# Eight small layers on one core: group routing in pieces inside the feed-forward, a norm's root on another engine, constants made in an earlier phase

## The reference

```python
# layer 1 feed-forward: 16 experts in 4 groups of 4, best 2 groups, best 4 experts
logits = xf @ router_w.T
scores = sigmoid(logits)
sb = scores + correction_bias
group_scores = top_k(sb.reshape(S, 4, 4), 2)[0].sum(-1)
group_idx = top_k(group_scores, 2)[1]
masked = where(score_mask > 0, sb, -inf)
topk_idx = top_k(masked, 4)[1]
w = take_along_axis(scores, topk_idx); w = w / (w.sum(-1) + 1e-20)
combine = zeros((S, 16)).at[arange(S)[:, None], topk_idx].add(w)
h = silu(xf @ gate_w) * (xf @ up_w)          # every expert, 32 columns each
out = shared + einsum('esh,ehc->sc', h * combine.T[:, :, None], down_w)

# layer 3 feed-forward: 8 experts, best 2, softmax of their probabilities
probs = softmax(x @ router); weights, indices = top_k(probs, 2); norm = softmax(weights)
```

## Time and profile before

| | us |
|---|---|
| median of 3 runs (lowest, highest) | 2025.56 (2020.61, 2027.13) |
| the profiled execution | 2014.69 |
| its span, first to last instruction | 2012.9 |
| TensorE busy, of the span | 1589.8 (79%) |
| VectorE busy | 1136.1 (56%) |
| ScalarE busy | 843.5 (42%) |
| GpSimd busy | 564.3 (28%) |

### The profile page before, as it was taken

The page is one execution under the profiler, slowest core; times in us unless marked ns, Lnnn a source line. Parts: engine busy times, 40 slices in busy tenths (PEclk is TensorE's granted clock), DMA queues, the critical chain, the costliest instruction groups (busy, mean ns, idle before and its releaser), DMA issues. The chain is left out here.

```text
span 2012.9 us, 46758 instructions
## 1 busy us (share of the span) xinstructions
PE 1589.8 (79%) x16783; PEld 1167.5 (58%) x16783; DVE 1136.1 (56%) x3048; ACT 843.5 (42%) x1634; POOL 564.3 (28%) x782
## 2 busy tenths in 40 slices
PE   4788999999488879699987776888887588353992
PEld 3655666666256647478875554555554488242882
DVE  5745677777445448356644576876674343552434
ACT  2422455555211115334432344655554476001763
POOL 4111011111101103422212211133233355374554
PEclk9989899999699989799997987998897799555996
DMA  4000222221099200000001002222220242221224
GB/s 173 1 2 10 65 57 61 55 55 44 8 286 328 91 0 1 1 3 3 3 3 64 1 1 58 66 68 66 64 71 21 64 113 86 71 74 45 78 78 144
DMA packets 84684, 124.99 MB, mean 62 GB/s; under 512 B 17329, under 2 KB 70577, under 8 KB 82929
## 3 DMA queue, kind: packets, MB, share of 16 engines
q1 hardware_dynamic: 75824, 104.30, 17.8%
q0 software_dynamic: 8640, 17.78, 2.5%
HBM read 67.47 MB, written 55.59 MB: 61 GB/s over the span
## 5 line engine op out<-in xcount | busy, mean ns | idle before, releaser
L1527 DVE TENSOR_REDUCE small<-ps 128x8 f32<-128x1024 f32 (+1 forms) x256 | 312.5, 1223 | 120.8 <-PE ps L1313 70.4
L1454 ACT ACTIVATE scr<-ps 128x1024 f32<-128x1024 f32 x256 | 262.0, 1023 | 239.7 <-PE ps L1288 121.2
L244 POOL TENSOR_TENSOR rstd<-vare,neghalf 128x4 f32<-128x4 f32 (+1 forms) x72 | 63.2, 878 | 543.6 <-DVE vare L223 542.2
L2826 POOL DMA_INDIRECT results<-scr x142 | 135.9, 957 | 143.8 <-DVE scr L2815 59.3
L1326 PE MATMUL ps<-scr 128*32 128x256 f32 x2048 | 174.0, 414 | 0.2 <-ACT scr L1454 0.2
L1275 PEld LDWEIGHTS ps<-scr_r 32*128 32x128 f32 x1024 | 82.3, 195 | 156.0 <-ACT scr L1454 88.8
L1275 PE MATMUL ps<-scr_r 32*128 32x256 f32 x1024 | 136.3, 344 | 35.8 <-ACT scr L1454 21.8
L2746 PE MATMUL ps<-scr 128*128 128x128 f32 x1136 | 153.4, 279 | 1.3 <-ACT scr L2773 1.3
L1306 PE MATMUL ps<-scr_r 32*128 32x256 f32 x1024 | 137.8, 351 | 10.0 <-DMA scr_r<-scr_r 5.5
L2746 PEld LDWEIGHTS ps<-scr 128*128 128x128 f32 x1136 | 141.9, 196 | 1.6 <-issue 1.6
L1911 PE MATMUL ps<-scr 64*64 64x64 f32 x4480 | 120.0, 223 | 13.3 <-DVE scr L2201 7.1
(11 more groups left out here) (410 smaller groups left out, 3547.7 us busy)
## 6 DMA issues: line engine op xcount, KB each, us to landing
scr_r<-scr_r SPq DMA_DIRECT2D x512, 64.0 KB
rows_m<-kinds SPq DMA_DIRECT2D x8, 2064.0 KB, 30.2
rows_f<-kinds SPq DMA_DIRECT2D x8, 2064.0 KB, 74.7
scr<-results SPq DMA_DIRECT2D x32, 256.0 KB
scr<-rows_m SPq DMA_DIRECT2D x71, 64.5 KB
scr<-rows_f SPq DMA_DIRECT2D x71, 64.5 KB
scr<-in_l3m SPq DMA_DIRECT2D x1, 3072.0 KB, 11.1
results<-scr POOLq DMA_INDIRECT x142
```

The costliest lines, as they stand in the source:

```text
L244: pool.tensor_tensor(k.rstd[:, 0:self.J], k.vare[:, 0:self.J], k.neghalf[:, 0:self.J], ALU.pow).then_inc(self.e["rstd_ready"].sem, 1)
L1454: act.activation(PT[:, g % 2, 2 * x:2 * x + 2, :], ps[:, 4:6, :], ACT.Exp).then_inc(e["prob_ready"].sem, 1)
L1527: dve.tensor_reduce(nf[:, half, 0:blocks, at:at + 2].rearrange("p q a -> p a q"), ps[:, 2 * (p % 2):2 * (p % 2) + 2, :].rearrange("p a (q ...
L2826: pool.indirect_dma_start(results, bass.IndirectOffsetOnAxis(ap=names[:, j % IN, P:P + 1], axis=0), y[:, j % OUT, :], None).then_inc(store ...
```

## The change

1. `phase_route_groups` and its phase are gone. A class `GroupRoute` does the same steps for one block of four tiles, in six pieces c=0 to 5. Block 0 is routed at the start of VectorE's part of the feed-forward, ahead of `make_spare`; block it+1 piece by piece behind the chunks of block it. The one sigmoid over all logits stays, and is now the first thing of ScalarE's part; it writes into `k.combine`, and the routing overwrites the scores there with the weights. GpSimd's `widen` waits for `routed` of its block.
2. Between the experts, `RootNorm` takes the place of `Norm`: ScalarE makes the square root, VectorE its reciprocal, in place of GpSimd's `pow`. On VectorE, normalise of block b moves from behind the names to right behind `choose` of block b-1.
3. The constants of the second `Dispatch` are made by VectorE inside the first expert phase, at tile 32, in place of the start of the stage between.

```diff
+class RootNorm(Norm):
+    def act_root(self, act, it):
+        k = self.k
+        act.wait_ge(self.e["var_ready"].sem, self.e["var_ready"].at(it))
+        act.activation(k.rstd[:, 0:self.J], k.vare[:, 0:self.J], ACT.Sqrt).then_inc(self.e["rstd_ready"].sem, 1)
+    def normalise(self, dve, it):
+        k = self.k
+        dve.wait_ge(self.e["rstd_ready"].sem, self.e["rstd_ready"].at(it))
+        dve.reciprocal(k.vare[:, 0:self.J], k.rstd[:, 0:self.J])
+        dve.drain()
+        if begun(it):
+            dve.wait_ge(self.e["turned"].sem, self.e["turned"].at(it - 1))
+        for j in range(self.J):
+            ins = dve.tensor_scalar(self.out(it, j), self.rows(it, j), k.mv[:, j, 0:1], k.vare[:, j:j + 1],
+                                    ALU.subtract, ALU.mult)
+        ins.then_inc(self.e["xn_ready"].sem, 1)
 # phase_ffn
     def act(act):
+        if route:
+            route.act(act)
     def dve(dve):
         def body(it, late):
                 if beside:
                     beside.dve(dve, it, c)
+                if route and it + 1 < NBLK:
+                    route.dve(dve, it + 1, c)
+        if route:
+            dve.wait_ge(k.arrive["l1f"], 16)
+            dve.wait_ge(route.scores_ready, 1)
+            for c in range(chunks):
+                route.dve(dve, 0, c)
         if begin:
             begin(dve)
     def widen(pool, it):
+        pool.wait_ge(route.e["routed"].sem, route.e["routed"].at(it))
         for c in range(routed):
-def phase_route_groups(k):
+class GroupRoute:
+    def act(self, act):
+        act.activation(self.k.combine[:, :, :], self.k.logits[:, :, :], ACT.Sigmoid).then_inc(self.scores_ready, 1)
+    def dve(self, dve, b, c):
+        k, sb, marked, won, top8, total, gs = self.k, self.sb, self.marked, self.won, self.top8, self.total, self.gs
+        score = k.combine[:, 4 * b:4 * b + 4, :]
+        if c == 0:
+            dve.tensor_tensor(sb, score, row4(k.w["l1f"]["bias"]), ALU.add)
+            dve.drain()
+            dve.tensor_tensor(self.hi, four[:, :, 0:2], four[:, :, 2:4], ALU.max)
+            dve.tensor_tensor(self.lo, four[:, :, 0:2], four[:, :, 2:4], ALU.min)
+            dve.drain()
+            dve.tensor_tensor(self.best, self.hi[:, :, 0:1], self.hi[:, :, 1:2], ALU.max)
+            dve.tensor_tensor(self.least, self.hi[:, :, 0:1], self.hi[:, :, 1:2], ALU.min)
+            dve.tensor_tensor(self.second, self.lo[:, :, 0:1], self.lo[:, :, 1:2], ALU.max)
+            dve.drain()
+        if c == 1:
+            dve.tensor_tensor(self.least, self.least, self.second, ALU.max)
+            dve.drain()
+            dve.tensor_tensor(gs.rearrange("p n g -> p (n g)"), self.best.rearrange("p n a -> p (n a)"),
+                              self.least.rearrange("p n a -> p (n a)"), ALU.add)
+            dve.drain()
+            dve.tensor_tensor(self.d1, gs[:, :, 0:3], gs[:, :, 1:4], ALU.is_ge)
+            dve.tensor_tensor(self.d2, gs[:, :, 0:2], gs[:, :, 2:4], ALU.is_ge)
+            dve.tensor_tensor(self.d3, gs[:, :, 0:1], gs[:, :, 3:4], ALU.is_ge)
+            dve.drain()
+        if c == 2:
+            code = row4(k.w["const"]["code4"])
+            dve.tensor_tensor(won[:, :, 0:3], self.d1, code[:, :, 0:3], ALU.subtract)
+            dve.memset(won[:, :, 3:4], -1.0)
+            dve.drain()
+            dve.tensor_tensor(won[:, :, 0:2], won[:, :, 0:2], self.d2, ALU.add)
+            dve.tensor_tensor(won[:, :, 2:4], won[:, :, 2:4], self.d2, ALU.subtract)
+            dve.drain()
+            dve.tensor_tensor(won[:, :, 1:4], won[:, :, 1:4], self.d1, ALU.subtract)
+            dve.drain()
+            dve.tensor_tensor(won[:, :, 0:1], won[:, :, 0:1], self.d3, ALU.add)
+            dve.tensor_tensor(won[:, :, 3:4], won[:, :, 3:4], self.d3, ALU.subtract)
+            dve.drain()
+        if c == 3:
+            dve.tensor_scalar(won, won, -2.0, -BIG, ALU.is_lt, ALU.mult)
+            dve.drain()
+            dve.tensor_tensor(four, four, spread_last(won.rearrange("p n g -> p (n g)"), 4), ALU.add)
+            dve.drain()
+            for t in range(4):
+                dve.max(top8[:, t, :], sb[:, t, :])
+            dve.drain()
+        if c == 4:
+            dve.memset(top8[:, :, 4:8], BIG)
+            dve.drain()
+            for t in range(4):
+                dve.match_replace(marked[:, t, :], top8[:, t, :], sb[:, t, :], 2.0 * BIG)
+            dve.drain()
+            dve.scalar_tensor_tensor(marked, marked, BIG, score, ALU.is_ge, ALU.mult)
+            dve.drain()
+        if c == 5:
+            dve.tensor_reduce(total[:, 0, :], marked, AX.X, ALU.add)
+            dve.drain()
+            dve.tensor_scalar_add(total[:, 0, :], total[:, 0, :], 1e-20)
+            dve.drain()
+            dve.reciprocal(total[:, 1, :], total[:, 0, :])
+            dve.drain()
+            dve.tensor_tensor(score, marked, spread_last(total[:, 1, :], 16), ALU.mult)
+            dve.drain().then_inc(self.e["routed"].sem, 1)
 # phase_sorted_experts, dve
+            if following and j == TILES:
+                following(dve)
 # phase_between
     def dve(dve):
-        d.prepare(dve)
         for b in range(NBLK + 2):
                 d.choose(dve, b - 1)
+            if b < NBLK:
+                ln.normalise(dve, b)
+            if 0 <= b - 1 < NBLK:
                 d.places(dve, b - 1, count)
                 d.name_by(dve, b - 1, 0)
             if 0 <= b - 2 < NBLK:
                 d.name_by(dve, b - 2, 1)
-            if b < NBLK:
-                ln.normalise(dve, b)
     def act(act):
         for b in range(NBLK):
+            ln.act_root(act, b)
             ln.act(act, b)
     def pool(pool):
         for b in range(NBLK + 2):
-            if b < NBLK:
-                ln.pool_rstd(pool, b)
```

More of the change, by code:

```diff
@@ L681, in phase_ffn @@
 def phase_ffn(k, w, chunks, per_y, func=ACT.Silu, b1=None, routed=0, comb=None, finish=None, ln=None,
-              pre=None, store=None, consts=None, begin=None, beside=None, opening=None):
+              pre=None, store=None, consts=None, begin=None, beside=None, opening=None, route=None):
     nc, ps = k.nc, k.ps
@@ L942, in spread_last @@
     return ap.rearrange("p (n a) -> p n a", a=1).broadcast_to([P, ap.shape[1], m])
-def phase_route_groups(k):
[L947 to L960, removed]
-        four = sb.rearrange("p n (g m) -> p (n g) m", m=4)
[L963 to L992, removed]
-        dve.tensor_scalar(won, won, -2.0, -BIG, ALU.is_lt, ALU.mult)
-        dve.drain()
-        dve.tensor_tensor(four, four, spread_last(won.rearrange("p n g -> p (n g)"), 4), ALU.add)
-        dve.drain()
-        for t in range(TILES):
-            dve.max(top8[:, t, :], sb[:, t, :])
-        dve.drain()
-        dve.memset(top8[:, :, 4:8], BIG)
-        dve.drain()
-        for t in range(TILES):
-            dve.match_replace(marked[:, t, :], top8[:, t, :], sb[:, t, :], 2.0 * BIG)
-        dve.drain()
-        dve.scalar_tensor_tensor(marked, marked, BIG, score, ALU.is_ge, ALU.mult)
-        dve.drain()
-        dve.tensor_reduce(total[:, 0, :], marked, AX.X, ALU.add)
-        dve.drain()
-        dve.tensor_scalar_add(total[:, 0, :], total[:, 0, :], 1e-20)
-        dve.drain()
-        dve.reciprocal(total[:, 1, :], total[:, 0, :])
-        dve.drain()
-        dve.tensor_tensor(k.combine[:, :, :], marked, spread_last(total[:, 1, :], 16), ALU.mult)
-    k.add_phase(act=act, dve=dve)
@@ L2676, in tables, with phase_sorted_experts @@
         dve.drain()
-def phase_sorted_experts(k, d, w, results, arrive, affine=None, scale=None, beside=None, load=None, pieces=1):
+def phase_sorted_experts(k, d, w, results, arrive, affine=None, scale=None, beside=None, load=None, pieces=1, following=None):
     ps, cst = k.ps, k.w["const"]
@@ L3000, in eight_layers @@
                                                   ln=ln0, consts=consts0, opening=opening))
-        phase_route_groups(k)
         w = k.w["l1f"]
@@ L3091, in eight_layers @@
         phase_sorted_experts(k, d, (both_of("l3m"), m["down"]), results, k.arrive["l3m"], affine=(w["g2"], w["be2"]),
-                             scale=ls2, beside=halted, load=late_load)
+                             scale=ls2, beside=halted, load=late_load, following=lambda dve: second.prepare(dve))
         g = Gathered(k, results, d.weights, X)
-        d = Dispatch(k, rows_f, two_weights(k.combine.rearrange("p t c -> p (t c)")[:, P:P + 64]), True)
-        phase_between(k, g, d, Norm(k, 4, 7, router=f["router"], tail_t=k.scr2[:, 8192:8704], natural=d.kept))
+        d = second = Dispatch(k, rows_f, two_weights(k.combine.rearrange("p t c -> p (t c)")[:, P:P + 64]), True)
+        phase_between(k, g, d, RootNorm(k, 4, 7, router=f["router"], tail_t=k.scr2[:, 8192:8704], natural=d.kept))
         phase_sorted_experts(k, d, (both_of("l3f"), f["down"]), results, k.arrive["l3f"], pieces=PIECES)
```

10 lines of the change are left out of this document (9 added, 1 removed).

## The result

The changed kernel took 2037.96 us (median of 10 runs, 2025.76 to 2045.92), the kernel before 2024.53 (10 runs, 2018.84 to 2030.5) on the same chip: ratio 1.0062, 95% interval 1.0036 to 1.0087. The profiled execution took 2027.6 us (span 2025.8), 12.9 more than that of before. The forecast was 2009.3.

What follows compares the result with a forecast made beforehand. VectorE's routing held TensorE before the feed-forward; between the experts, a four-engine chain was paced later by GpSimd's indirect DMAs. 9.1 + 8.4 - 1.2 = 16.3 us gain, 2009.3 us forecast, range 2002 to 2020.

Steps and rivals of the forecast that it cites:

- First product: Feed-forward start: routing only block 0 first brings the first hidden product from 553.45 to 540.95, gaining 12.5 us.
- Cold TensorE: Feed-forward opening: TensorE starts at half clock and a second slow step could follow, costing 0.7 us (0 to 2.8).
- The seven other blocks: Feed-forward: routing pieces overrun VectorE's idle time by 0.4 us in four blocks and 2.3 in two, costing 2.7.
- Part 1: Routing moved into the feed-forward: 12.5 gained, 0.7 and 2.7 lost, +9.1 us in all.
- The rival's 3 us for a late fetch of code: Feed-forward: dearer routing pieces and a longer VectorE program give 2015.7 us, 2020 with a few late fetches; chance 0.12.
- Constants: First experts after tile 32: making the second dispatch's constants there gains and costs nothing, 0 us (-1.9 to 0).
- The loop: Between the experts: normalise runs beside the ranking, GpSimd's scatters set 10.1 to 10.5 us per block, gain 8.4 us.
- The first scatter: Between the experts: block 0's root takes 1.7 us against 1.04 on GpSimd, so the first scatter is 0.65 late.
- The rival's 10.97 us per block: Between the experts: normalise doesn't fit under the ranking, the loop stays unchanged, gain 2.7 us, 2015.0 in all; chance 0.13.
- GpSimd's queue becomes the bound: Between the experts: eight scatters per block take 10.1 to 10.5 us, above VectorE's 9.7, so they pace the loop; +8.4.
- GpSimd's writes and VectorE share time: Between the experts: one possible reason for normalise not fitting under the ranking, gain 2.7 instead of 8.4 us; chance 0.13.
- Silu's table: Second experts' start: the root's table stands where Silu's was, so the first Silu waits for a load, costing 1.2 us.

Runs made afterwards that it cites:

- prompt sets: Sets of runs in which the kernel before took 1954.1 and 1951.1 us and no result was read late; the changed kernel's ratio there was 0.9911.
- late sets: Sets of runs in which the kernel before took 2017.7 to 2023.3 us, like at first; the changed kernel's ratio there was 1.0062 and 1.0064.
- dead_pow: Changed kernel plus an idle four-element pow on GpSimd ahead of each block's eight scatters; ratio 0.9972 to the kernel before, first to last scatter stretch 112.3 us.
- set 2: Second of five sets of follow-up runs, each on one chip; the kernel before took 1951.1 us, the changed kernel had ratio 0.9911.
- set 3: Third of five sets of follow-up runs, each on one chip; the kernel before took 2023.3 us there.
- between_alone: Changed kernel with the old routing phase restored, keeping the three edits between and beside the experts; ratio 0.9951 to the kernel before.
- pow_by_gpsimd: Changed kernel with 1/deviation again made by GpSimd's pow, the new VectorE order kept; ratio 0.9978 to the kernel before.
- constants_home: Changed kernel with the second dispatch's constants made at the start of the stage between the experts again; ratio 1.0057 to the kernel before.
- after_third: The changed kernel itself, run once more for comparison on one chip; ratio 1.0064 to the kernel before.
- order_twice: Changed kernel with normalise again at the end of VectorE's block, root and reciprocal kept as changed, second run; ratio 1.0001 to the kernel before.
- route_second: Routing inside the feed-forward as changed, stage between the experts as before, run a second time; ratio 0.9953 to the kernel before.
- step_each_four: Changed kernel plus a 0.19 us addition and a drain on GpSimd after every four scatters; ratio 1.0024 to the kernel before.

## Why the prediction was wrong

Step by step, in its order:

- **First product**: 10.5 us after the first routing instruction, measured 10.2; block 0's routing with its spare-row preamble as sized. Gain 12.5 forecast, 12.8 measured.
- **Cold TensorE**: 0.7 forecast; the gain shrinks from 12.8 at the first product to 12.1 at block 0's residual add.
- **The seven other blocks**: 24.5 forecast for blocks 1 and 2, measured 24.32 and 24.70; 23.49, then 23.39 to 23.40 for the others. 2.7 forecast, 2.4 measured. The granted clock from block 2 on is 1.00 (2.4 GHz) in both kernels; over the whole feed-forward, with its opening, it is 0.98, before 0.99. Part 1 is 9.7 for 9.1. (The rival's 3 us for a late fetch of code comes from no row, and blocks of 23.39 to 23.49 us leave room for none.)
- **Constants**: 0 forecast, 129.3 against 129.5 measured.
- **The loop**: the mechanism was right in prompt sets, and its sum within 1 us: scatters unbroken from the second group on, 1.267 us each, so 10.1 us per eight as forecast, and router results 9.6 to 9.9 apart; first to last 101.6 where the forecast's times make 102.5 (1728.19 to 1831.7, less the last scatter's 0.96). The first scatter was 1.1 us later, not 0.65. (The rival's 10.97 us per block is 10.92 by the two times that it names; this touches no term of the sum.)
- **The step that failed**: "GpSimd's queue becomes the bound", term +8.4, measured -18.5 in late sets. I treated a full queue on GpSimd as a bound on GpSimd alone. What stood in its place: results of TensorE and VectorE seen late beside a long run of scatters, 33 us in all, of which some lay beside the scatters anyway. The pow that I counted as a cost of 1.04 us and a gap per block was worth more than it cost there: dead_pow puts it back, idle, and the loop is 17 us shorter. It kept the runs to eight scatters, and the old phase kept the transposes and the router within the first 5 us of a run (done 2.3 and 4.9 us after its start in block 4); but the ranking, 9.8 us into it, was on time as well, so this account of why is argued and not complete. Nothing in my rivals had it; the nearest, "GpSimd's writes and VectorE share time", was priced at a gain of 2.7 us. The sign was in the trace: 20.2 us of "remote" before L1454, beside other scatters. I never asked what those were.
- **Silu's table**: 1.2 forecast, 0.15 measured: last scatter to first Silu 15.82 us (15.67 before), with the load of 1.28 us in it. ScalarE has room there. The Trainium skill's 1.38 us of drain with each load ("ScalarE: Activation LUTs", What ACT_TABLE_LOAD costs) doesn't show: the root starts at 1725.88, 0.02 after its load of 1.28 us from 1724.58 ends. Nor is it ahead of a load: Silu's starts at 1864.41, 0.02 after the copy before it.

The range of 2002 to 2020 was too narrow for another reason too: it was built from one condition of the chip. The same pair of kernels gives 0.9911 in one set and 1.0062 or 1.0064 in others.

**What stays open.** What makes a set late or prompt isn't known; no experiment changed it. It isn't fixed to the chip: the records give chip 11 for set 2, which is prompt, and for set 3, which is late. Nor is the mechanism known. That an idle instruction, a wait or a drain in GpSimd's run takes part or all of the lateness away in late sets is shown; by what the run holds back the others, and why the kernel before escapes it with runs of eight, is not. Leaving the second four scatters out wasn't tried. between_alone and pow_by_gpsimd weren't run in a late set, so that the lateness needs nothing of the routing part, and that the new order with a pow in use is free of it, is not shown. dead_pow and the route alone were not compared with the changed kernel on one chip, constants_home and after_third were the ones that stood in for it.

## What to carry to other kernels

Taking work off an engine that issues transfers in software changes the rhythm of its queue, not only its load: ask what now runs back to back, and who completes work beside it. Idle time "remote" in the profile of before, beside such a queue, is a price that a change can multiply; look at it before forecasting. And where the rows of before carry such a sign, measure the change in more than one set of runs before believing either number.

## What the runs showed of the hardware

- In late sets, results of TensorE that are ready 9 us into a run of 12 or 16 of GpSimd's indirect DMAs are read 2 to 5 us late, and those of 15 to 17 us into a run of 16 only 2.8 us after its end (2.81, 2.80 and 2.80 us in the first profile). VectorE's drained steps stretch from 1.46 us to 2.0 to 2.8 in order_twice. The scatters themselves keep their pace, 0.96 us plus 0.30.
- The run's length alone doesn't decide: beside the runs of eight of the kernel before and of route_second, with a pow in use between them, nothing is late 9.8 us into the run, also in late sets.
- In prompt sets 60 scatters in a row delay nothing.
- A gap of 1.33 us with an idle pow behind every eight scatters takes 20 of 33 us of lateness away from the 16 results, and adds 8.6 to the ranking's; another instruction of 0.2 us behind every four (gap 0.39 to 0.54) takes 10.
- A drain on GpSimd behind four scatters and a small addition is followed by 2.0 to 2.2 us, once by 3.48, in which its queue stands (step_each_four).
- The same kernel took 1951 to 1954 us in some sets and 2018 to 2025 in others. Between its two profiled executions (2014.69 and 1959.55) some 22 us lie in layer 3's attention and what leads to the first experts, 20 in the first experts (143.9 and 124.3) and 15 in the second (145.6 and 130.6, to the first addition behind them), all stages in which GpSimd issues indirect DMAs beside TensorE.
